# A four-layer graph network on one core: the row maxima of attention in one transfer, and a second pass in another order

## The reference

```python
h = jnp.maximum(_layernorm(x, axis=-1), 0.0)
x = x + _L0_gnn_ref(h, adj, ...)   # normalised graph convolution, batch norm over all graphs
h = jnp.maximum(_layernorm(x, axis=-1), 0.0)
x = x + _L1_gnn_ref(h, adj, ...)   # 8 heads of 32: softmax(mask(Q K^T / sqrt(32))) V, then Wo
h = jnp.maximum(_layernorm(x, axis=-1), 0.0)
x = x + _L2_gnn_ref(h, adj, ...)   # adj @ h, W1 to 1024, rms norm, silu, W2
h = jnp.maximum(_layernorm(x, axis=-1), 0.0)
x = x + _L3_gnn_ref(h, adj, ...)   # 4 heads of 64: softmax(mask(leaky(e_i + e_j))) @ (h W)
```

## Time and profile before

| | |
|---|---|
| runs | 3989.51, 3992.93 and 3992.46 us, median 3992.46 |
| the profiled execution | 3984.56 us, its span 3982.8 us |
| TensorE busy | 3709.5 us, 93% of the span |
| VectorE busy | 3101.9 us, 78% |
| ScalarE busy | 1994.8 us, 50% |
| GpSimd busy | 1576.2 us, 40% |
| mean clock granted to TensorE | 0.953 |

### The profile page before, as it was taken

One profiled execution on the slowest core, in us unless ns is written; L12 is line 12 of the kernel. 1 busy time (PEld: TensorE's weight loads), 2 busy tenths in 40 slices (PEclk: granted clock), 3 DMA queues, 4 the chain that ended last, 5 costly groups with the idle time before them and its releaser, 6 DMA issues.

```text
span 3982.8 us, 59433 instructions
## 1 busy us (share of the span) xinstructions
PE 3709.5 (93%) x19042; PEld 2707.6 (68%) x19042; DVE 3101.9 (78%) x5637; ACT 1994.8 (50%) x3047; POOL 1576.2 (40%) x980
## 2 busy tenths in 40 slices
PE   7999579999999999999999999999999999999986
PEld 6888346676667766666666676766677666666665
DVE  6787557888887888888888888888878888888752
ACT  4656145555555555555545545555555555555430
POOL 4667234333443444444433333334434444444310
PEclk9999689999999999999999999999999999999986
DMA  8988322222222212222222222222222212222200
GB/s 286 317 310 298 93 53 64 70 69 69 63 58 69 60 52 56 53 69 69 69 69 69 69 69 69 69 69 63 58 69 59 58 52 53 69 69 69 53 16 11
DMA packets 195935, 341.10 MB, mean 86 GB/s; under 512 B 28720, under 2 KB 64432, under 8 KB 195888
## 3 DMA queue, kind: packets, MB, share of 16 engines
q1 hardware_dynamic: 195888, 340.50, 30.3%
HBM read 188.89 MB, written 50.33 MB: 60 GB/s over the span
## 4 chain that ended last, share of the span: by engine, by line
PE 78%; DVE 10%; ACT 4%; issue 3%; POOL 2%; DMA 2%; SPq 1%; DVEq 0%; ACTq 0%; POOLq 0%
PE bank L1444 12%; PE bank L1495 12%; PE obank L1378 12%; PE bank L1233 9%; PE pair L1233 7%; PE pair L1362 7%; PE bank L1406 6%; PE bank L1463 3%; PE pair L1339 3%; DVE minus_max L1033 2%; PE obank L1265 2%; DMA pT<-in_adjT 2%; PE bank L1265 1%; DVE b_st L841 1%; ACT hsq L632 1%
## 5 line engine op out<-in xcount | busy, mean ns | idle before, releaser
L602 POOL TENSOR_TENSOR pT<-pT,node_edge 128x1024 f32<-128x1024 f32 x256 | 628.6, 2462 | 532.0 <-ACT pT L690 530.1
L690 ACT ACTIVATE pT<-pair 128x1024 f32<-128x1024 f32 x512 | 515.9, 1031 | 325.6 <-PE obank L1378 248.2
L1033 DVE TENSOR_REDUCE minus_max<-pair 128x2 f32<-128x1024 f32 x512 | 603.3, 1216 | 56.9 <-PE pair L1339 56.5
L1023 DVE TENSOR_TENSOR pT<-pT,node_edge 128x1024 f32<-128x1024 f32 x256 | 399.8, 1562 | 269.4 <-ACT pT L690 266.2
L1495 PEld LDWEIGHTS bank<-v,p3T 128*128 128x128 f32 x4096 | 502.4, 199 | 36.2 <-DVE p3T L1182 24.5
L1495 PE MATMUL bank<-v,p3T 128*128 128x65 f32 x4096 | 499.8, 280 | 20.2 <-DVE p3T L1182 20.2
L540 POOL TENSOR_TENSOR d_rs<-d_ve,minus_half 128x4 f32<-128x4 f32 x32 | 32.2, 1007 | 1207.5 <-DVE d_ve L853 1207.5
L1378 PE MATMUL obank<-pT,v 128*64 128x512 f32 x2048 | 490.3, 611 | 8.4 <-POOL pT L602 4.8
L1444 PE MATMUL bank<-w_s,hid 128*128 128x256 f32 x2048 | 479.6, 389 | 0.3 <-DVE hid L1112 0.3
L1444 PEld LDWEIGHTS bank<-w_s,hid 128*128 128x128 f32 x2048 | 383.6, 192 | 87.7 <-issue 40.1
L632 ACT ACTIVATE p3T<-x,d_sh,d_rs 128x256 f32<-128x256 f32 x128 | 66.4, 589 | 720.6 <-POOL d_sh L546 720.6
...
## 6 DMA issues: line engine op xcount, KB each, us to landing
...
q_parts<-high_parts SPq DMA_DIRECT2D x256, 128.0 KB, 4.7
k_parts<-high_parts SPq DMA_DIRECT2D x256, 128.0 KB, 4.1
...
```

Of the source, the lines that this page charges most:

```text
L602: nc.gpsimd.tensor_tensor(half, half, node_edge[:, 0:2, :], ALU.mult).then_inc(a_masked[0].sem, 1)
L690: nc.scalar.activation(dst, pair[p][:, :, :], func, **more).then_inc(a_copied[p].sem, 1)
L1023: nc.vector.tensor_tensor(half, half, node_edge[:, 2:4, :], ALU.mult).then_inc(a_masked[1].sem, 1)
L1033: nc.vector.tensor_reduce(minus_max[:, t, 2 * two_heads:2 * two_heads + 2], pair[p][:, :, :], AX.X, ALU.max, negate=True).then_inc(a_copie ...
```

## The change

First, `a.putshift` sends the eight rows of maxima with one transfer and not with eight, and `a.scores` waits for one and not eight. Source and target bytes are the same.

Second, the table `ORDER` is replaced. All lags of ScalarE, VectorE, TensorE and GpSimd are one larger; on SyncE some are. The lags are relative, so most of this is only another place for the cut between steps. What is left is a number of places at which tasks swap on an engine. The step written as a loop runs 27 times and not 28, with one more written-out step on each side.

```diff
 ORDER = """
-a.exp00:2 a.max11:1 a.max20:1 a.scores11:1 b.hid3:2 b.hidc1:3 a.exp01:2 a.max21:1 b.rrms:3 b.hidc2:3 a.scores20:1
...
+a.scores10:2 a.div1:3 b.hid2:3 b.hid3:3 a.scores11:2 a.mask7:3 a.exp10:3 b.hidc2:4 b.rstd3:4 b.hid4:3 a.max20:2
...
-        a_shift_in = signal("a_shift_in", H1, 16)
+        a_shift_in = signal("a_shift_in", 1, 16)
...
             def put_shift(g):
                 sp.wait_ge(*o_copied.upto(g, 1))
-                for h in range(H1):
-                    sp.dma_start(q_parts[ROW_SHIFT:ROW_SHIFT + 1, h, :].bitcast(f32),
-                                 shiftT[h:h + 1, :].bitcast(f32)).then_inc(a_shift_in.sem, 16)
+                sp.dma_start(q_parts[ROW_SHIFT:ROW_SHIFT + 1, :, :].bitcast(f32),
+                             shiftT[:, :].bitcast(f32)).then_inc(a_shift_in.sem, 16)
...
-                    pe.wait_ge(*a_shift_in.upto(g, H1))
+                    pe.wait_ge(*a_shift_in.upto(g, 1))
```

More of the change, by code:

```diff
@@ L68 @@
 ORDER = """
-a.exp00:2 a.max11:1 a.max20:1 a.scores11:1 b.hid3:2 b.hidc1:3 a.exp01:2 a.max21:1 b.rrms:3 b.hidc2:3 a.scores20:1
-a.scores21:1 a.mask6:2 b.eye:2 a.max30:1 h.spread0:3 b.hid4:2 a.max31:1 b.x30:3 a.values00:1 a.values01:1 a.scores30:1
-b.x31:3 h.values00:3 a.exp10:2 a.exp11:2 b.stats3:3 a.mask7:2 h.values01:3 a.scores31:1 a.exp20:2 b.hidc3:3 a.exp21:2
-b.hid5:2 h.spread1:3 a.scores40:1 a.scores41:1 b.hid6:2 b.hidc4:3 b.rstd3:3 a.xmid0:2 p.sortk:1 a.exp30:2 b.hid7:2
-a.exp31:2 a.values10:1 a.values11:1 a.scores50:1 b.hidc5:3 a.max40:1 h.values10:3 a.max41:1 h.values11:3 a.headc0:2
@@ L74 @@
-a.xmid1:2 a.max50:1 a.max51:1 a.scores51:1 b.sum:2 a.scores60:1 h.spread2:3 b.rstd:2 b.hidc6:3 a.values20:1 b.bias:2
-a.bias:1 b.hidc7:3 b.stats:2 a.mask0:1 a.mask1:1 a.exp40:2 a.max60:1 a.load:0 a.scores61:1 a.values21:1 a.scores70:1
-a.exp41:2 a.exp50:2 a.max61:1 h.values20:3 b.factors:3 b.spread:2 a.headc1:2 a.scores71:1 b.sumsq1:2 p.flip:0
-h.values21:3 a.max70:1 a.exp51:2 a.exp60:2 p.norm:1 a.max71:1 a.values30:1 h.spread3:3 a.values31:1 b.sumsq2:2
-a.exp61:2 b.low:3 b.vcol:3 b.aggl0:2 a.putshift:1 a.mask2:1 a.exp70:2 p.q0:0 b.aggl1:2 b.v3c0:3 a.edges1:1 p.q1:0
@@ L84 @@
-b.flip31:2 a.div0:1 b.diag:2 a.nat61:0 b.e:2 a.vmask6:1 a.nat70:0 b.sumsq7:2 b.scale0:2 b.scale1:2 a.vmask7:1
-h.head2:3 a.nat71:0 p.flipl:0 b.scale2:2 b.flip3c0:3 h.prob3:3 b.agg0:1 b.flip3c1:3 a.mask4:1 a.shift:0 b.silu0:2
-b.silu1:2 b.scale3:2 b.vt:2 b.agg1:1 b.norm:2 b.v30:2 p.qlow:0 b.hid0:1 b.hid1:1 a.scores00:0 b.load:1 h.store:3
-b.silu2:2 b.silu3:2 b.exps:3 p.klow:0 a.scores01:0 b.hid2:1 b.aggc0:2 a.div1:1 a.mask5:1 a.load1:0 b.v31:2
-a.scores10:0 a.shiftc:1 p.rstd:0 a.max00:0 a.max01:0 b.edges:2 b.aggc1:2 a.max10:0 b.hidc0:2 p.sortq:0 a.edges0:0
@@ L89 @@
-h.head3:3
+a.scores10:2 a.div1:3 b.hid2:3 b.hid3:3 a.scores11:2 a.mask7:3 a.exp10:3 b.hidc2:4 b.rstd3:4 b.hid4:3 a.max20:2
+a.max21:2 h.store:4 a.max30:2 a.max31:2 b.x30:4 h.spread0:4 b.hid5:3 a.scores20:2 b.hid6:3 b.hidc3:4 b.x31:4
+a.scores21:2 b.hidc4:4 a.values00:2 a.exp11:3 a.values01:2 b.hidc5:4 a.scores30:2 h.values00:4 b.stats3:4 a.xmid0:3
+a.max40:2 a.scores31:2 h.values01:4 a.max41:2 a.exp20:3 b.hid7:3 a.scores40:2 h.spread1:4 a.values10:2 b.hidc6:4
+a.values11:2 a.exp21:3 a.exp30:3 a.scores41:2 a.scores50:2 a.xmid1:3 a.max50:2 a.headc0:3 a.bias:2 b.stats:3 a.max51:2
@@ new lines @@
+a.max60:2 h.values10:4 b.rstd:3 h.values11:4 b.eye:3 a.scores51:2 b.bias:3 p.norm:2 a.load:0 a.exp31:3 p.sortk:1
+b.factors:4 b.hidc7:4 a.exp40:3 a.exp41:3 a.scores60:2 b.sum:3 h.spread2:4 a.exp50:3 a.headc1:3 a.max61:2 a.max70:2
+a.edges1:2 a.scores61:2 a.load0:0 a.exp51:3 a.exp60:3 b.aggl0:3 b.vcol:4 a.mask0:2 a.max71:2 a.values20:2 b.sumsq1:3
+b.sumsq2:3 a.exp61:3 a.values21:2 h.values20:4 a.scores70:2 a.exp70:3 a.mask1:2 b.spread:3 b.sumsq3:3 h.values21:4
+a.scores71:2 a.putshift:1 b.aggl1:3 b.v3c0:4 p.rstd:1 p.x1:1 a.headc2:3 b.low:4 b.v3c1:4 a.vmask0:2 p.flip:1
@@ new lines @@
+b.norm:3 b.exps:4 a.nat41:1 a.wo1:2 b.aggc0:3 b.aggc1:3 a.nat50:1 a.nat51:1 b.sumsq7:3 a.mask4:2 b.scale1:3 h.head2:4
+a.vmask7:2 p.flipl:1 a.mask5:2 b.flip30:3 a.nat60:1 h.prob3:4 b.scale2:3 b.scale3:3 b.silu0:3 b.flip31:3 b.e:3
+a.shiftc:2 a.nat61:1 p.qlow:1 b.silu1:3 b.silu2:3 a.nat70:1 b.hidc0:3 p.klow:1 b.agg0:2 b.vt:3 a.nat71:1 b.silu3:3
+b.agg1:2 b.edges:3 a.shift:1 b.v30:3 a.exp00:2 a.edges0:1 a.exp01:2 a.max00:1 b.hid0:2 b.rrms:3 b.hidc1:3 a.scores00:1
+a.scores01:1 a.max01:1 a.max10:1 a.max11:1 h.head3:4 b.hid1:2 b.v31:3 b.load:1 a.load1:0 p.sortq:0 a.mask6:2
```

10 lines of the change are left out of this document (5 added, 5 removed).

## The result

| | before | after |
|---|---|---|
| median of 4 runs each | 3990.99 us | 4094.79 us |
| lowest and highest | 3987.18, 3992.93 | 4084.38, 4103.99 |
| ratio, 95% interval | | 1.0261 (1.0235 to 1.0287) |
| the profiled execution | 3984.56 us, span 3982.8 | 4094.48 us, span 4092.2 |

The changed kernel is 2.6% slower, 104 us. The forecast was 3974 us, so the sign was wrong and the time lies outside the range.

A forecast was written before the change was run, and what follows sets the result against it. Bound: the chain from x_mid through statistics and norm to TensorE's aggregation. -0.5 us a graph over some 30 graphs (-15), first graph -4.5, drain +1.5: -18 us, so 3974 us median; own range 3958 to 3990, wider range 3942 to 4010.

The forecast's parts named there:

- Step 5: Remaining moves (hidden parts, keys' sort, output store, silu parts): hand-offs stay in time, costed at nothing.
- Step 1: VectorE takes x_mid's statistics after one maximum, not two: aggregation 1.15 us earlier, product moved +0.4, net -0.8 us a graph.
- Step 2: Turn of the maxima goes behind the aggregation's second half on TensorE: its wait goes, -0.3 us a graph.
- Step 3: Scores after the late turn, with one transfer: sum takes no wait; page-based estimate 0.2 us a graph.
- Step 4: ScalarE does the next graph's input norm before exp31, so values11 wait for VectorE's mask: +0.6 us a graph.
- The ends: First graph: -4.5 us, first scores near 480.5; drain of the last graph: +1.5 us.
- A: Rival: gain given back by another late task or hand-offs; graph at 0, about 3989 us; chance 0.20.
- C: Rival: longer single idle before the aggregation makes it start at 1.2 GHz; 3992 to 4025 us; chance 0.12.
- D: Rival: the one transfer lands at 4.7 us, scores wait 2.7 us a graph; about 4055 us; chance 0.08.
- B: Rival: shorter TensorE waits bring every graph to full clock, 1.1 us a graph more; 3941 us; chance 0.10.

The follow-up runs named there:

- both losses undone: Changed kernel with a.div0 again ahead of b.diag on VectorE and the output store again ahead of the queries' sort: 3974.08 us, ratio 0.9965.
- the run with eight transfers: Changed kernel with division first, store early and p.norm back between head 6's exponentials, but the maxima sent in eight transfers: 4137.10 us, ratio 1.0352.

## Why the prediction was wrong, step by step

The bound was read rightly: the chain from x_mid to the aggregation, and the region between the output product and the turn. Nothing of the loss arose there. It arose at two places that the sum put at nothing.

**Step 5, "The other moves I cost at nothing", failed.** It costs 121 us.
- The swap of `b.diag` and `a.div0` is not in its list at all. By the two tables, 50 pairs of VectorE's tasks change places, and this is one of them. At the durations of the kernel before it is worth 0.87 us: the division ended at 2090.57 there, and the copy behind it waited for nothing and began at 2091.44. So I would have cost it at nothing even had I named it. What was missing is that a duration on VectorE depends on what GpSimd does. The trace of before held it. In the first graph the same multiply took 1.91 us, beside a mask:

```profile
517.14 1.91 DVE L1047 TENSOR_TENSOR att1T<-att1T,rden 128x512 f32<-128x512 f32 x1
```

```profile
516.37 2.14 POOL L602 TENSOR_TENSOR pT<-pT,node_edge 128x1024 f32<-128x1024 f32 x1 [2.05 <-ACT pT L690]
```

  And the mean of VectorE's own mask, 1555 ns in the earlier trace rows where many take 1.23 us, told of the same: in the kernel before, 66 of these masks start in the middle of one of GpSimd, last 1.4 to 3.0 us, and end 1.1 us behind it. The Trainium skill's page "SBUF — State Buffer" (section "Who interferes with whom") states it: a VectorE instruction with two SBUF inputs, or one in a two-port mode, is blocked for the whole of a GpSimd instruction that reads SBUF and started first. By that rule the trace agrees: the multiply that started at 2034.17 ended 0.5 us behind the mask's end at 2036.08. The prediction cites this page for its port figure only, and not for this.
- "The store of the output ... lands about 2 us before x3 is written again." The issue came at 2066.95, 7.0 us ahead of b.x3's start at 2073.93, and b.x3 would have started at 2072.80 without its wait. But the landing was taken as the 3.2 us of before, where the store went ahead of the sort. Behind twelve transfers of 128 KB it took 6.8 us. With 3.2 it would have been 2.6 us early.

**Step 1 had the right mechanism and was mis-sized.** It gave the earlier statistics 1.15 us a graph, less 0.4 for the product that moves. The chain is shorter as forecast: from the end of x_mid to the aggregation it is 7.9 us on the mean before, 6.9 with both losses undone. With the rest in place the worth of the earlier statistics is 106.12 - 104.46 = 1.66 us: 0.9 of idle time, the rest from matmuls that are less often slow. In the old order it is worth nothing, since a score product then waits for its maximum.

**Step 2 was right as to the wait.** The turn waits no longer; in the list of the changed kernel's waits there is none for L1349. No run has this move alone, so its worth in time is not shown.

**Step 3 was right.** In each graph from the third on the scores start 2.4 us after the copy, with under 0.1 us of wait. The landing itself is not in the trace, but the start of the scores tells of it. In the second graph TensorE waits 0.5 us, and they start 2.35 us after the issue, as in all later graphs (2.35 to 2.37); in the run with eight transfers, where they wait 3.9 us, they start 1.75 to 1.83 us after the last issue. So the single transfer takes some 0.55 us longer than the last of the old ones. The prediction's estimate of 0.5 us from the Trainium skill's pages agrees with that, and the 0.2 us of wait that it made of it measured 0.07. What I did not say is how much the new order leans on it: 183 us with eight transfers.

**Step 4 was right in kind and nearly in size.** +0.6 us was taken; the wait is 0.46 us and the period changes by 0.71.

**The ends were wrong.** The first scores start at 487.00 and not near 480.5:

```profile
487.00 2.04 PE L1360 MATMUL pair<-q_parts,k_parts 97*128 97x512 f32 x4 [4.90 <-issue]
```

The wait shrank by 3.0 us, not by the 4.5 of the sum, and the first pass ended 3.6 us later in this execution (the first opening load is at 421.0, before at 417.4). Counted from that load, the turn of the maxima comes 1.2 us later than before and the first scores 1.8 us earlier, not 4.5. The last part, from the opening load of the last graph at 3723.1 to the end at 4092.2, takes 369 us against 353 before (3629.9 in the earlier trace rows to 3982.8); with both losses undone it is 361. So this part costs some 8 us more than before, where the sum has 1.5 for the drain.

**The rivals.** None named either mechanism, and the chances for slower, 0.22 in all, lay on other causes. A, a gain given back through hand-offs, was nearest in kind; it put the worst at 0. C and D gave the sign, not the cause: the clock follows the waits here and does not come first, and the transfer was innocent. B came true in part in the kernel with both undone: its clock is 0.99, and its period 0.65 us below that of the kernel before although its idle time is 0.3 us longer. The wait that B took to be untouched, that of the second output product, fell from 1.48 to 1.08 us, and the product was slow in none of the graphs, where it had been in 14 of 26. That 3974 was both forecast and measured for that kernel is partly chance: the graph gains 0.65 us and not 0.5, and the drain loses more.

**What stays open.** Why the wait of the second output product is shorter in the new order was not taken apart, nor why the terms of layer 3 run slow in some graphs of a kernel and not in others. The first opening load lies between 417 and 428 us in the profiled executions of this study; what moves it was not looked into either.
